# First attention with its first 128 tokens ahead, and the router's scores in two parts

## The chip, the cores and the metric

One core of a Trainium2 chip runs the kernel. The metric is device time in microseconds, the median over executions. The profile is of one further execution, and its times are counted from the start of its span. PE is TensorE, DVE is VectorE, ACT is ScalarE, POOL is GpSimd, SP is SyncE.

## What is computed

The reference takes x of 2 x 1024 x 128 through two blocks, each a mixer and a feed-forward part, with a modulated layer norm ahead of each part. All is float32.

```
h = layernorm(x)*(1+ca)+sa;  x = x + ga*spikes(h)        # RWKV-like scan, then a membrane with threshold
h = layernorm(x)*(1+cb)+sb;  x = x + gb*transformer(h)   # 2 layers: shifted tokens, 8 heads of 64, window 64, GLU
h = layernorm(x)*(1+ca)+sa;  x = x + ga*lru(h)           # second block: linear recurrence
h = layernorm(x)*(1+cb)+sb;  x = x + gb*moe(h)           # shared expert + 8 experts, top 2 by sigmoid score
q = l2norm(q)*q_scale; k = l2norm(k)*k_scale             # inside attention, then rotary with scaling
shift_token(t): features 64..127 come from the token before
```

## The kernel before

The 2,048 tokens are held feature-major (features in partitions) in four groups of 512, and token-major in 16 tiles of 128. Every engine runs one program in the order in which it is written, and semaphores tie them together. Nothing is planned at run time: an instruction that waits holds up all behind it on its engine.

The change touches two places.

**The ramp into the first attention.** VectorE has run the membrane passes and turns the membrane states into spikes with `threshold(g)` (compare, then multiply by the gate, 512 columns), groups 0 to 2 ahead of a branch on a fallback, group 3 later. `add_spikes(g)` adds them to x: groups 0 and 1 on VectorE, 2 and 3 on GpSimd. TensorE turns each group token-major (`stack_t1`). For the layer norm VectorE takes statistics (`ln_stats`: four BATCH_NORM rows, then the negated mean at L1012 and the variance plus epsilon at L1013), GpSimd computes the power -0.5 (`ln_rstd`, L715) and the negated mean times it (L716), ScalarE normalises four tiles (`ln_norm`, L412), TensorE turns them back (`ln_t2`), and ScalarE writes z with the modulation (`stack_out`, L418). For group 0 VectorE copies z into hsA, lower half straight and upper half shifted by one token (`shifted`, L1193 and L1195); DMAs do that for groups 1 to 3. From hsA, TensorE makes k and q of a tile (`proj_part`, L1596) and v (`proj_v`, L1651). VectorE makes the rotary products (L1211, L1214), ScalarE squares, VectorE sums and clamps them (L1225, L1232), and GpSimd computes the power -0.5 of the 16 sums (`norms`, L909) and scales k (`k_normed`, L917), while VectorE scales q (L1240). TensorE then turns q and k (`turn_qk`, L1507), and scores, exponentials and the product with v follow. `keep_clock(n)` is n products of constants that nothing reads.

```
proj_v(0, 0); proj_part(0, 2, 1); keep_clock(3, psT1[:, :]); turn_qk(0, 0); proj_part(0, 2, 0)
# proj_v, first tile:
pe.wait_ge(s["ln_norm"], TPG * (ln_no(1, NG - 1) + 1))
```

`norms(0)` belongs to tile 0 of the first attention. Its later tiles overlap three deep: while tile i is weighed, i+1 is scored, i+2 turned, and i+3 projected.

**The router.** After its scores are through the sigmoid, `compare_scores` compares the eight scores of each token pairwise on VectorE (is_equal and is_gt, 1,024 columns each, L1451), GpSimd combines the two results, and `weigh_experts` (L1457 to L1470, twelve VectorE steps) makes the gates. Between them VectorE makes the products of the shared expert (`shared_hidden(k)`, L1423, eight in all) for which TensorE waits, group by group, and copies each group's result (L1481). TensorE opens each group's result by turning x into it (L1971), and then adds the shared expert (L1976).

## Time and profile before

| what | us |
|---|---|
| median of 3 runs | 549.89 |
| lowest and highest | 549.76, 549.9 |
| the profiled execution | 550.24 |
| its span | 548.4 |
| PE busy, DVE busy in the span | 491.0, 424.6 |
| ACT busy, POOL busy in the span | 348.8, 339.6 |

A busy PE is not PE at its peak, since matmuls are pipelined. What counts for a change is which engine's wait ends last in the stretch that it touches, so the rows below are of stretches and not of the whole.

### The profile page before, as it was taken

How to read it: one execution, taken by the hardware profiler on the slowest of the kernel's cores; microseconds unless marked ns; L12 is line 12 of the kernel's file. 1: busy time of each engine (PE TensorE's matmuls, PEld its weight loads, DVE VectorE, ACT ScalarE, POOL GpSimd, SP SyncE). 2: the span in 40 equal slices, each digit the busy share in tenths (PEclk: the TensorE clock that was granted, in tenths of full speed). 3: DMA queues.
4: the chain of work that ended last, by engine and by line, in shares of the span. 5: the costliest groups of instructions: out<-in, count | busy, mean ns of one | idle time of the engine just before them, and what ended most of it. 6: DMA issues, size and time to landing. Idle time of an engine off the chain costs nothing.

```text
span 548.4 us, 11780 instructions
## 1 busy us (share of the span) xinstructions
PE 491.0 (90%) x4047; PEld 312.7 (57%) x4047; DVE 424.6 (77%) x1172; ACT 348.8 (64%) x999; POOL 339.6 (62%) x271
## 2 busy tenths in 40 slices
PE   5753078999999999999899999999999999999996
PEld 5333033567777776443367777777544445667775
DVE  6899999898899875566889988995545687466665
ACT  5762007689999987433689999998565536433332
POOL 5990018999999997667999999993101277410000
PEclk9875579999999999999999999999999999999999
DMA  9600003311111112000221111111000000000000
GB/s 306 232 2 1 0 2 96 68 31 41 41 40 39 39 35 78 0 1 1 70 57 39 33 40 39 41 41 31 0 2 0 1 0 1 1 1 19 22 19 20
DMA packets 15024, 20.98 MB, mean 38 GB/s; under 512 B 2378, under 2 KB 9012, under 8 KB 14708
## 3 DMA queue, kind: packets, MB, share of 16 engines
q1 hardware_dynamic: 14676, 20.13, 13.3%
q8 instruction: 33, 0.54, 0.4%
q14 instruction: 27, 0.22, 0.1%
q10 hardware_dynamic: 288, 0.08, 0.1%
HBM read 9.99 MB, written 1.05 MB: 20 GB/s over the span
## 4 chain that ended last, share of the span: by engine, by line
PE 67%; DVE 16%; POOL 8%; issue 4%; ACT 3%; DMA 1%; DVEq 0%; SPq 0%; POOLq 0%; ACTq 0%
PE psT L1507 11%; PE psQK L1596 8%; PE psO L1719 6%; PE psO L1651 5%; PE psQK L1926 5%; PE psS L1699 4%; DVE vst L1106 3%; DVE vAB L1110 3%; PE psO L1507 3%; POOL rn L909 3%; PE psS L1998 3%; PE psQK L1733 3%; PE psS L1835 3%; PE psO L1998 2%; PE psQK L1858 2%
## 5 line engine op out<-in xcount | busy, mean ns | idle before, releaser
L575 ACT ACTIVATE prob<-psS,nmx 128x128 f32<-128x128 f32 x256 | 90.1, 377 | 18.0 <-DVE nmx L1246 18.0
L909 POOL TENSOR_TENSOR rn<-ssq,half 128x16 f32<-128x16 f32 x32 | 93.2, 2912 | 6.8 <-DVE ssq L1232 6.7
L901 POOL TENSOR_TENSOR ra<-ra,rb 128x512 f32<-128x512 f32 x64 | 80.6, 1280 | 1.0 <-DVE rb L1214 0.8
L715 POOL TENSOR_TENSOR rst<-mv,half 128x4 f32<-128x4 f32 x24 | 25.7, 1072 | 73.8 <-DVE mv L1013 64.0
L1596 PE MATMUL psQK<-wqkv,hsA 128*128 128x512 f32 x128 | 61.2, 596 | 0.9 <-DVE hsA L1195 0.6
L575 ACT ACTIVATION_READ_ACCUMULATOR prob<-psS,nmx 128x1 f32 x256 | 55.1, 215 | 0.0
L917 POOL TENSOR_TENSOR qkn<-ra,rn 128x512 f32<-128x512 f32 x32 | 49.6, 1549 | 2.5
L1211 DVE TENSOR_TENSOR ra<-psQK,rope 128x512 f32<-128x512 f32 x64 | 43.9, 685 | 9.4 <-PE psQK L1596 8.9
L1214 DVE TENSOR_TENSOR rb<-psQK,rope 128x512 f32<-128x512 f32 x64 | 43.5, 679 | 0.0
L696 ACT ACTIVATE gel<-psQK 128x512 f32<-128x512 f32 x32 | 19.1, 597 | 37.5 <-PE psQK L1926 37.5
L1225 DVE TENSOR_REDUCE ssq<-sq 128x8 f32<-128x512 f32 x64 | 41.0, 676 | 1.6 <-ACT sq L515 1.3
L1246 DVE TENSOR_REDUCE nmx<-psS 128x4 f32<-128x512 f32 x64 | 41.0, 682 | 0.7 <-PE psS L1699 0.7
L1507 PEld LDWEIGHTS psT<-ident,qkn 128*128 128x128 f32 x256 | 29.6, 141 | 20.5 <-issue 14.5
L1507 PEld LDWEIGHTS psT<-ident,prob 128*128 128x128 f32 x256 | 29.9, 140 | 15.9 <-issue 15.4
L1719 PE MATMUL psO<-vAB,pT 128*64 128x64 f32 x1024 | 36.9, 225 | 0.0
L549 ACT ACTIVATE pT<-psT 128x512 f32<-128x512 f32 x64 | 36.3, 648 | 0.7 <-PE psT L1507 0.7
L1507 PE MATMUL psT<-ident,qkn 128*128 128x128 f32 x256 | 34.0, 274 | 2.6 <-DVE qkn L1240 2.0
L1719 PEld LDWEIGHTS psO<-vAB,pT 128*64 128x64 f32 x1024 | 32.4, 138 | 6.8 <-issue 4.6
L1651 PE MATMUL psO<-wqkv,hsA 128*128 128x512 f32 x64 | 35.7, 640 | 0.0
L412 ACT ACTIVATE lnx<-psS,nmr,rst 128x128 f32<-128x128 f32 x20 | 7.5, 457 | 43.6 <-POOL nmr L716 43.6
L1699 PE MATMUL psS<-kT,qT 64*64 64x128 f32 x1024 | 33.4, 269 | 0.0
L1351 DVE SCALAR_TENSOR_TENSOR hg<-psO,vec,gel 128x512 f32<-128x512 f32 (+1 forms) x24 | 17.2, 745 | 20.9 <-ACT gel L628 20.9
(262 smaller groups left out, 1183.8 us busy)
## 6 DMA issues: line engine op xcount, KB each, us to landing
vAB<-vAB SPq DMA_DIRECT2D x62, 128.0 KB, 2.2
wqkv<-in_wqkv SPq DMA_DIRECT2D x2, 768.0 KB, 8.4
big<-in_x SPq DMA_DIRECT2D x4, 256.0 KB, 4.8
ra<-in_rope_t SPq DMA_DIRECT2D x1, 1024.0 KB, 7.3
ropeb<-in_rope SPq DMA_DIRECT2D x1, 1024.0 KB, 8.6
big<-in_ew SPq DMA_DIRECT2D x2, 512.0 KB, 4.1
wmod<-in_wmod SPq DMA_DIRECT2D x2, 384.0 KB, 6.9
out<-big SPq DMA_DIRECT2D x3, 256.0 KB, 2.3
```

The costliest lines, as they stand in the source:

```text
L575: act.activation(prob[:, k, :], psS[:, hb, c * P:(c + 1) * P], ACT.Exp, bias=nmx[:, k:k + 1], accum_out=sums[:, n % 2, k:k + 1]).then_inc( ...
L901: pool.tensor_tensor(o, o, rb[:, r], ALU.add).then_inc(s["sum_" + name], 1)
L909: pool.tensor_tensor(rn[:, :], ssq[:, :], half[:, :], ALU.pow).then_inc(s["rn_ready"], 1)
L917: pool.tensor_tensor(heads(qkn[:, INNER:]), heads(ra_k[n % 2]), rn[:, 8:16].unsqueeze(2).to_broadcast([P, H, DH]), ALU.mult).then_inc(s["k ...
L1211: dve.tensor_tensor(heads(o), heads(psQK[:, part, :]), rope[:, at8, 2 * part, :].unsqueeze(1).to_broadcast([P, H, DH]), ALU.mult).then_inc ...
L1214: dve.tensor_tensor(rb[:, r].rearrange("p (h a d) -> p h a d", h=H, a=2), psQK[:, part, :].rearrange("p (h a d) -> p h a d", h=H, a=2)[:, ...
L1225: dve.tensor_reduce(ssq[:, 8 * part:8 * part + 8], heads(sq[:, part * INNER:(part + 1) * INNER]), AX.X, ALU.add).then_inc(s["ssq_" + name], 1)
L1507: i = pe.transpose(dst[:, k * P:(k + 1) * P], src(k), ident[:, :])
L1596: mm(psQK[:, part, :], hsA[:, tile(i)], wqkv[:, part * INNER:(part + 1) * INNER], start=True, stop=True).then_inc(s[name + "_mm"], 1)
L1651: mm(psO[:, 1, :], hsA[:, tile(i)], wqkv[:, 2 * INNER:3 * INNER], start=True, stop=True).then_inc(s["v_fill"], 1)
L1699: j = mm(psS[64 * w:64 * w + 64, e, c * P:(c + 1) * P], qT[r, c, 64 * w:64 * w + 64], keys, start=False, stop=True, skip_group_check=True)
L1719: j = mm(psO[64 * w:64 * w + 64, 0, h * DH:(h + 1) * DH], pT[:, slot(h), 64 * w:64 * w + 64], (vA, vB)[w][:, u, h * DH:(h + 1) * DH], star ...
```

## The change

Group 0 of the first layer norm is taken in two steps. ScalarE computes its power as exp(-0.5 ln v), normalises two tiles, and as soon as TensorE has turned the first tile (into psQK) it writes z for tokens 0 to 127; VectorE copies these into hsA, and the first k product starts from them. The other three tiles are turned behind that product, and z and hsA for tokens 128 to 511 follow. The power of tile 0's sums (`norms(0)`) moves from GpSimd to ScalarE in the same way, ahead of the normalisation of group 3; the table set with ln and exp is loaded beforehand. Thresholds 2 and 3 move from VectorE to GpSimd, each ahead of its add. Several steps of all four engines change places: ScalarE's first squares of k come ahead of group 2's normalisation, VectorE's statistics of groups 2 and 3 come later, GpSimd's rstd of group 3 comes between the two rotary sums of tile 0, and TensorE's turn of group 3 comes behind the q product. Of the ten and four clock-keeping products there, four, two and four remain.

In the router, is_gt moves behind the fourth product of the shared expert, GpSimd's multiply waits for is_equal alone, and `weigh_experts` is cut in two: seven steps (`choose_experts`) after the sixth product, five ahead of the eighth. The copy of group 2's result moves behind the eighth.

```
@@ -498,6 +498,7 @@
     act.wait_ge(s["table"], 1)
+    act.preload_act_table_set("natural_log_exp_and_others")
     load_table(ACT.Exp)
...
@@ -519,13 +520,45 @@
         ln_out(ln_no(1, g), z[:, gsl(g)], mod[:, 0, CB, b:b + 1], mod[:, 0, SB, b:b + 1])
-    ln_norm(ln_no(1, 0))
-    stack_out(0)
+    def power(dst, src):
+        own.one(act.activation(dst, src, ACT.Ln, bias=0.0, scale=1.0))
+        return act.activation(dst, dst, ACT.Exp, bias=0.0, scale=-0.5)
+    def first_norm():
+        n = ln_no(1, 0)
+        act.wait_ge(s["ln_var"], n + 1)
+        power(rst[:, n % 4, :], mv[:, n % 4, :, 1]).then_inc(s["rst_act"], 1)
+        act.wait_ge(s["rst_act"], 1)
+        act.wait_ge(s["ln_rstd"], n + 1)
+        act.wait_ge(s["ln_t2"], n - 1)
+        for k in range(TPG):
+            act.activation(lnx[:, n % 2, k, :], stat_bank(n)[:, k, :], ACT.Identity, bias=nmr[:, n % 4, k:k + 1],
+                           scale=rst[:, n % 4, k:k + 1]).then_inc(s["ln_norm"], 1)
+            if k == 1:
+                act.wait_ge(s["first_t2"], 1)
+                act.activation(z[:, 0:P], psQK[:, 0, 0:P], ACT.Identity, bias=mod[:, 0, SB, 0:1],
+                               scale=mod[:, 0, CB, 0:1]).then_inc(s["first_out"], 1)
+        act.wait_ge(s["ln_t2"], n + 1)
+        act.activation(z[:, P:GW], out_bank(n)[:, P:GW], ACT.Identity, bias=mod[:, 0, SB, 0:1],
+                       scale=mod[:, 0, CB, 0:1]).then_inc(s["ln_out"], 1)
+    def norms(n):
+        act.wait_ge(s["ssq_max"], n + 1)
+        if n:
+            act.wait_ge(s["k_ready"], n)
+            act.wait_ge(s["q_ready"], n)
+        power(rn[:, :], ssq[:, :]).then_inc(s["rn_ready"], 1)
+    first_norm()
     ln_norm(ln_no(1, 1))
+    squares_k(0)
     ln_norm(ln_no(1, 2))
     stack_out(1)
-    squares_k(0)
     squares_q(0)
+    norms(0)
     ln_norm(ln_no(1, 3))
@@ -878,16 +911,19 @@
     def add_spikes(g):
+        own.one(pool.tensor_scalar(by_chunk(ekv, g), of_group(ph, g, 1), -1.0, mod[:, 0, GA, bof(g):bof(g) + 1],
+                                   ALU.is_lt, ALU.mult))
         pool.wait_ge(s["x_mixed"], g)
-        if g == 3:
-            pool.wait_ge(s["spk"], 1)
         pool.tensor_tensor(x_cm[:, gsl(g)], x_cm[:, gsl(g)], ekv[:, gsl(g)], ALU.add).then_inc(s["x_mixed"], 1)
+    pool.wait_ge(s["x_mixed"], 1)
     add_spikes(2)
-    ln_rstd(ln_no(1, 0))
+    n = ln_no(1, 0)
+    pool.wait_ge(s["rst_act"], 1)
+    pool.tensor_tensor(nmr[:, n % 4, :], nmean[:, n % 4, :], rst[:, n % 4, :], ALU.mult).then_inc(s["ln_rstd"], 1)
     add_spikes(3)
-    for g in range(1, NG):
-        ln_rstd(ln_no(1, g))
+    ln_rstd(ln_no(1, 1))
+    ln_rstd(ln_no(1, 2))
     def heads(x):
...
@@ -921,10 +957,13 @@
         if has(i + 2):
-            norms(n + 2)
+            if n + 2:
+                norms(n + 2)
             k_normed(n + 2)
...
             rope_sum(n + 3, 1)
+            if n + 3 == 0:
+                ln_rstd(ln_no(1, 3))
             rope_sum(n + 3, 0)
...
@@ -990,8 +1029,9 @@
     pool.tensor_tensor(ew2g[0], ew2, gate(0, NE), ALU.mult).then_inc(s["wg_ready"], 1)
+    pool.wait_ge(s["pairs_ready"], 1)
+    own.one(pool.tensor_tensor(big4, big4, before[:, :, :].unsqueeze(1).to_broadcast(sh4), ALU.mult))
     pool.wait_ge(s["pairs_ready"], 2)
-    own.one(pool.tensor_tensor(big4, big4, before[:, :, :].unsqueeze(1).to_broadcast(sh4), ALU.mult))
     pool.tensor_tensor(big4, big4, big5, ALU.add).then_inc(s["better_ready"], 1)
...
@@ -1151,7 +1191,6 @@
     threshold(own, 1)
-    threshold(own, 2)
     changed = dve.value_load(cnti[0:1, 0:1], min_val=0, max_val=P * B * NCH)
...
@@ -1170,7 +1209,7 @@
         renewed = Steps(dve, s["renewed"])
-        for g in range(NG - 1):
+        for g in range(2):
             threshold(renewed, g)
...
@@ -1183,9 +1222,7 @@
     ln(ln_no(1, 0))
-    threshold(Steps(dve, s["spk"]), 3)
     ln(ln_no(1, 1))
-    ln(ln_no(1, 2))
     def shifted(dst, src, g, name):
@@ -1265,14 +1302,23 @@
         clamped(n)
+    dve.wait_ge(s["first_out"], 1)
+    dve.tensor_copy(hsA[0:64, 0:P], z[0:64, 0:P]).then_inc(s["hsA_first"], 1)
+    dve.tensor_copy(hsA[64:128, 1:P + 1], z[64:128, 0:P]).then_inc(s["hsA_first"], 1)
+    ln(ln_no(1, 2))
     dve.wait_ge(s["ln_out"], ln_no(1, 0) + 1)
-    shifted(hsA, z, 0, "hsA_ready")
+    dve.tensor_copy(hsA[0:64, P:GW], z[0:64, P:GW]).then_inc(s["hsA_ready"], 1)
+    dve.tensor_copy(hsA[64:128, P + 1:GW + 1], z[64:128, P:GW]).then_inc(s["hsA_ready"], 1)
+    dve.wait_ge(s["rope_ready"], 4)
+    rope_products(0, 1)
     ln(ln_no(1, 3))
-    dve.wait_ge(s["rope_ready"], 4)
-    qk_first(0)
+    rope_products(0, 0)
+    sum_squares(0, 1)
+    sum_squares(0, 0)
+    clamped(0)
     rope_products(1, 1)
+    q_normed(0)
     rope_products(1, 0)
-    q_normed(0)
     def mid(l, g):
@@ -1447,22 +1493,30 @@
         own.one(dve.tensor_tensor(sel, sg, rbias[:, :].unsqueeze(1).to_broadcast([P, NT, NE]), ALU.add))
-        for pairs, op in ((big4, ALU.is_equal), (big5, ALU.is_gt)):
-            dve.tensor_tensor(pairs, sel.unsqueeze(2).to_broadcast(sh4), sel.unsqueeze(3).to_broadcast(sh4),
-                              op).then_inc(s["pairs_ready"], 1)
-    def weigh_experts():
+        dve.tensor_tensor(big4, sel.unsqueeze(2).to_broadcast(sh4), sel.unsqueeze(3).to_broadcast(sh4),
+                          ALU.is_equal).then_inc(s["pairs_ready"], 1)
+    def compare_greater():
+        dve.tensor_tensor(big5, sel.unsqueeze(2).to_broadcast(sh4), sel.unsqueeze(3).to_broadcast(sh4),
+                          ALU.is_gt).then_inc(s["pairs_ready"], 1)
+    dn2 = sq[:, 3 * P + NT:3 * P + 2 * NT]
+    dn3 = sq[:, 3 * P + 2 * NT:3 * P + 3 * NT]
+    def choose_experts():
         dve.wait_ge(s["better_ready"], 1)
...
         own.one(dve.tensor_reduce(den, comb, AX.X, ALU.add))
-        dn2 = sq[:, 3 * P + NT:3 * P + 2 * NT]
-        dn3 = sq[:, 3 * P + 2 * NT:3 * P + 3 * NT]
         own.did(dve.tensor_scalar(dn2, den, 1e-9, None, ALU.is_gt))
...
         own.one(dve.reciprocal(den, den))
+    def weigh_experts():
         own.one(dve.tensor_tensor(den, den, dn2, ALU.mult))
...
@@ -1472,13 +1526,19 @@
         for k in range(max(2 * g, 2), 2 * g + 2):
+            if k == 2 * NG - 1:
+                weigh_experts()
             shared_hidden(k)
...
                 compare_scores()
+            elif k == 3:
+                compare_greater()
         if g == 2:
-            weigh_experts()
-        dve.wait_ge(s["ey_done"], g + 1)
-        dve.tensor_copy(big[:, 4, gsl(g)], (psT0, psT1)[g % 2][:, :]).then_inc(s["ey_used"], 1)
+            choose_experts()
+        else:
+            for m in ((g - 1, g) if g == NG - 1 else (g,)):
+                dve.wait_ge(s["ey_done"], m + 1)
+                dve.tensor_copy(big[:, 4, gsl(m)], (psT0, psT1)[m % 2][:, :]).then_inc(s["ey_used"], 1)
     dve.wait_ge(s["ey_used"], NG)
...
@@ -1589,7 +1649,10 @@
         name = "qk"[part]
-        stacked(l, i)
+        if n:
+            stacked(l, i)
+        else:
+            pe.wait_ge(s["hsA_first"], 2)
         if n:
...
@@ -1625,18 +1688,26 @@
     stack_t1(1)
+    keep_clock(4, psT1[:, :])
     stack_t1(2)
-    keep_clock(10, psT1[:, :])
-    ln_t2(ln_no(1, 0))
-    stack_t1(3)
+    keep_clock(2, psT1[:, :])
+    first = ln_no(1, 0)
+    pe.wait_ge(s["ln_norm"], TPG * first + 1)
+    pe.transpose(psQK[:, 0, 0:P], lnx[:, first % 2, 0, :], ident[:, :]).then_inc(s["first_t2"], 1)
     keep_clock(4, psT1[:, :])
...
     proj_part(0, 0, 1)
+    pe.wait_ge(s["ln_norm"], TPG * (first + 1))
+    for k in range(1, TPG):
+        i = pe.transpose(out_bank(first)[:, k * P:(k + 1) * P], lnx[:, first % 2, k, :], ident[:, :])
+    i.then_inc(s["ln_t2"], 1)
+    proj_part(0, 0, 0)
+    stack_t1(3)
     ln_t2(ln_no(1, 1))
-    proj_part(0, 0, 0)
+    proj_part(0, 1, 1)
     ln_t2(ln_no(1, 2))
-    proj_qk(0, 1)
+    proj_part(0, 1, 0)
     keep_clock(4, psT1[:, :])
```

## Rows read from the trace of the kernel before

**Rows 1.** The page: the chain that ended last, shares of the span by engine.
```profile
PE 67%; DVE 16%; POOL 8%; issue 4%; ACT 3%; DMA 1%; DVEq 0%; SPq 0%; POOLq 0%; ACTq 0%
```

**Rows 2.** Timeline of VectorE from 77.8 us: start, length, engine, line, operation, tiles, count, idle.
```profile
77.92 1.29 DVE L1180 TENSOR_TENSOR x_cm<-x_cm,big 128x512 f32<-128x512 f32 x2 [0.27 <-DVE big L1147]
...
80.84 0.16 DVE L1013 TENSOR_SCALAR mv<-mv 128x4 f32<-128x4 f32 x1
...
82.85 1.17 DVE L1012 TENSOR_SCALAR nmean<-mv 128x4 f32<-128x4 f32 x1
```

**Rows 3.** Timeline of GpSimd, 77.8 to 83 us.
```profile
79.36 1.26 POOL L884 TENSOR_TENSOR x_cm<-x_cm,big 128x512 f32<-128x512 f32 x1 [36.85 <-DVE x_cm L1180]
...
82.58 0.20 POOL L716 TENSOR_TENSOR nmr<-nmean,rst 128x4 f32<-128x4 f32 x1
82.73 1.26 POOL L884 TENSOR_TENSOR x_cm<-x_cm,big 128x512 f32<-128x512 f32 x1
```

**Rows 4.** The chain that ended last, 76.2 to 78.7 us: start, length, what.
```profile
77.32 0.53 issue
```

**Rows 5.** Timeline of GpSimd, 209 to 220.5 us.
```profile
209.78 3.87 POOL L826 TENSOR_SCALAR tsin<-big 128x1024 f32<-128x1024 f32 x1
...
218.96 1.16 POOL L826 TENSOR_SCALAR tsin<-big,fr 128x1024 f32<-128x1024 f32 x1
```

**Rows 6.** Timeline of VectorE in the same stretch.
```profile
209.72 0.42 DVE L1193 COPY big<-z 64x512 f32<-64x512 f32 x1
210.17 1.15 DVE L1195 COPY big<-z 64x512 f32<-64x512 f32 x1
```

**Rows 7.** Timelines of ScalarE, 5 to 22 us and 82.5 to 98 us.
```profile
12.92 0.19 ACT L474 ACTIVATE sc<-fr 128x3 f32<-128x3 f32 x1
...
82.81 1.50 ACT L412 ACTIVATE lnx<-psS,nmr,rst 128x128 f32<-128x128 f32 x4 [35.41 <-POOL nmr L716]
85.06 0.78 ACT L418 ACTIVATE z<-psO,mod 128x512 f32<-128x512 f32 x1 [0.75 <-PE psO L1507]
...
91.27 1.50 ACT L412 ACTIVATE lnx<-psO,nmr,rst 128x128 f32<-128x128 f32 x4
```

**Rows 8.** Timeline of VectorE, 104 to 113.5 us.
```profile
105.78 0.67 DVE L1232 TENSOR_SCALAR ssq<-ssq 128x16 f32<-128x16 f32 x1
```

**Rows 9.** Timeline of GpSimd, 88 to 114 us.
```profile
92.46 2.91 POOL L909 TENSOR_TENSOR rn<-ssq,half 128x16 f32<-128x16 f32 x1 [0.28 <-DVE ssq L1232]
...
106.53 2.91 POOL L909 TENSOR_TENSOR rn<-ssq,half 128x16 f32<-128x16 f32 x1
```

**Rows 10.** Timeline of TensorE, 84 to 98.5 us.
```profile
86.90 1.10 PE L1596 MATMUL psQK<-wqkv,hsA 128*128 128x512 f32 x2 [0.57 <-DVE hsA L1195]
...
93.32 1.02 PE L1651 MATMUL psO<-wqkv,hsA 128*128 128x512 f32 x2
...
97.05 0.65 PE L1507 MATMUL psT<-ident,qkn 128*128 128x128 f32 x4 [0.24 <-POOL qkn L917]
```

**Rows 11.** Timeline of VectorE, 470 to 487.5 us.
```profile
473.47 1.22 DVE L1451 TENSOR_TENSOR rb<-sq 128x1024 f32<-128x1024 f32 x1
...
483.20 0.17 DVE L1466 TENSOR_TENSOR sq<-sq 128x16 f32<-128x16 f32 x1
...
484.14 0.29 DVE L1470 TENSOR_TENSOR sq<-sq 128x128 f32<-128x128 f32 x1
...
485.08 1.28 DVE L1423 TENSOR_TENSOR hg<-psO,gel 128x512 f32<-128x512 f32 x2
```

**Rows 12.** Timeline of TensorE, 470 to 489 us.
```profile
474.07 1.02 PE L1920 MATMUL psO<-hsA,wsh 128*128 128x512 f32 x2
475.34 0.66 PE L1971 MATMUL psT<-ident,x_cm 128*128 128x128 f32 x4 [0.24 <-DVE hg L1423]
...
486.41 0.66 PE L1971 MATMUL psT<-ident,x_cm 128*128 128x128 f32 x4 [0.39 <-DVE hg L1423]
```

**Rows 13.** The chain that ended last, 468 to 490 us.
```profile
483.44 0.86 PE psS L1919 x2
```

More of the change, by code:

```diff
@@ L193, in program @@
             kv_mm num_ready ek_ready gek_ready ekv_ready sb_ready den_ready r_mm r_ready cur_ready x_mixed
-            rope_scaled rope_turned td_ready kbias halves scales eps_ready seed_ln seed_ready newton_ready rough_ready quot_ready
+            rst_act first_t2 first_out hsA_first rope_scaled rope_turned td_ready kbias halves scales eps_ready seed_ln seed_ready newton_ready rough_ready quot_ready
             dve dve_b act_own pool_own fallback fallback_b rope_ready tabs_phase tabs_ready z_ready hsA_ready
```

## The prediction

> **What bounds the kernel now.** I read the page first. The chain that ended last is two thirds TensorE [rows 1], so a gain counts only where TensorE waits. There are two such places under the change: the ramp into the first attention, and the router. Next I read the timelines of VectorE, GpSimd, ScalarE and TensorE from 77.8 us on, as one sequence. VectorE adds spikes to the first two groups from 77.92, the first being done at about 78.6 [rows 2]. GpSimd adds the third group from 79.36 to 80.62. The first group's variance is ready at 81.00; GpSimd raises it to the power -0.5 and multiplies, and ScalarE normalises from 82.81 [rows 2, 7]. TensorE turns all four tiles, ScalarE writes z from 85.06 to 85.84 [rows 7], VectorE copies it into hsA, and the first product starts at 86.90, 0.15 after the copies end at 86.75 [rows 10]. Tile 0's clamp is done at about 92.38, GpSimd's power follows from 92.46 to 95.37 [rows 9], TensorE turns tile 0's q and then its k, the latter at 97.05 [rows 10]. The reader should see which queue has something behind each wait.
>
> **Removing threshold 2 from VectorE: nothing.** The instruction is about 0.65 us, as an add of the same columns is (1.29 for two), but VectorE is already idle for 0.27 us before its first add [rows 2]. The chain shows 0.53 us of issue there [rows 4], just behind the branch on the fallback. The branch path sets the start, and the branch does not wait for threshold 2. Bounds: 0, and a gain of 0.65 if reading the branch's value turns out to queue behind it. I take 0.
>
> **Thresholds 2 and 3 on GpSimd: 1.9 us each.** No row shows this pair of operations there. The nearest are tensor-scalar instructions on 1,024 columns: 1.16 us for multiply and add, 3.87 us for add and add [rows 5]. Halved for 512 columns that is 0.58 and 1.94. Compare-and-multiply is not multiply-and-add, so I take 1.9. [...]
>
> **What that does to the first variance: +1.1.** Threshold 2 starts at 78.6 + 0.15 = 78.76 and ends at 80.66; the third add then runs to 82.0 instead of 80.62. VectorE's negated mean falls at 80.76, inside that add. The trace has the same meeting: a negated mean, as small as the variance of 0.16, took 1.17 from 82.85 and ended at 84.02, as GpSimd's add of 82.73 ended at 83.99 [rows 2, 3]. So the variance is ready at 82.1, not 81.00.
>
> **Ln and Exp for the first power: -1.0.** From variance to normalising takes 81.00 to 82.81 = 1.81 before. After, it is two small ScalarE instructions of 0.19 [rows 7], the multiply on GpSimd of 0.20 [rows 3] and 0.22 of handovers between them, 0.80 in all. Normalising starts at 82.1 + 0.8 = 82.9: the saving pays for the collision and no more.
>
> **The first 128 tokens: a product 0.45 to 2.35 us earlier.** One normalisation is 1.50 / 4 = 0.375 [rows 7], one turn with handovers about 0.35, one small z about 0.4: z's first 128 columns are there at 84.05. GpSimd is then in threshold 3 (82.9 to 84.8), with its fourth add behind it (84.85 to 86.1). The two copies to hsA are VectorE copies, and a copy beside GpSimd's 3.87 us instruction took 1.15 instead of 0.42 [rows 6]: held, but not to the end of it. Three outcomes: both pass during threshold 3 (copies done 84.4), both pass as it ends (85.05), or the second falls behind the fourth add (86.3). The product starts 0.15 later: 84.55, 85.2 or 86.45, against 86.90.
>
> **The rest of the group: later.** The three other turns now stand in TensorE's queue behind that product, and ScalarE waits for them with everything behind it. Product 0.86, turns 0.55, z for 384 columns 0.65: z is whole 2.07 after the product starts, at 86.6, 87.3 or 88.5, against 85.84. The two larger copies (0.72) end at 87.35, 88.0 or 89.25, against 86.75. From there to the clamp VectorE does the same instructions as before (the statistics of group 3, four rotary products, two sums): 92.38 - 86.75 = 5.63, so 93.0, 93.65 or 94.9.
>
> **Tile 0's power on ScalarE: 2.4 saved, and not reached.** Ln and Exp take about 0.45 instead of 2.91 [rows 7, 9]: done at 93.45, 94.1 or 95.35, against 95.37. But the normalisation of group 3 stands behind them on ScalarE (1.50), and ends at 95.0, 95.65 or 96.9, where it ended at 91.27 + 1.50 = 92.77 before [rows 7]. The first v product (93.32 before [rows 10]) waits for it, and in TensorE's queue that product, a k product and three clock-keeping products (0.86 + 0.86 + 0.65) stand ahead of the turn of q. So the turn of q comes at 97.4, 98.1 or 99.35, and that of k 0.44 behind it: 0.8, 1.45 or 2.75 later than 97.05. The saved 2.4 us lie under this wait.
>
> **What reaches the steady state: +0.3, +0.95 or +2.25.** Tile 2's power started at 106.53 as GpSimd came free [rows 9]. Its clamp was drawn out to 0.67 from 105.78 [rows 8], where so small an instruction takes 0.16 [rows 2]: 0.5 us of room. The rest passes on, since TensorE is then nearly full to the end of the layer. I take the middle of the first two, +0.6.
>
> **Router: -0.7.** TensorE is free at 474.93 (474.07 + 0.86, the step of such a product in the chain [rows 13]) and waits for VectorE's fourth product until 475.34, because the second comparison (1.22) stands ahead of that product [rows 11, 12]. With the comparison behind it, the product can start at 473.5 or as soon as its SiLU is there, 0.64 us: no wait is left, -0.41. GpSimd's multiply starts a comparison earlier, so its two results are not late. At the last group TensorE waits until 486.41. There VectorE first ends five weighing steps (483.20 to 484.43), a copy, then two products (485.08, 1.28) [rows 11]. After the change the first product starts when TensorE's third group ends (483.44 - 0.41 = 483.03 [rows 13]), then 0.64, five steps of 1.23 together, 0.68 and handovers: 485.65, and TensorE goes on at 485.7, -0.7 in all. Bounds: -0.41, and -0.41 - 0.39 = -0.8, the idle time before that row [rows 12].
>
> **Sum.** +0.6 - 0.7 = -0.1. The profiled execution took 550.24 us (548.4 of span and 1.84 around it), which gives 550.1; it stands 0.35 over the median of the runs, 549.89, so I forecast 549.8.
>
> **Rivals.**
> *Slower: the first copies fall behind the fourth add.* For it: the negated mean of 82.85 and the copy of 210.17 each let GpSimd's instruction go on [rows 2, 6]. Against it: both may slip through at 84.8. It decides if the second copy asks for its data after threshold 3 ends and the add has begun. Attention +2.25, router -0.7: +1.55, a median of 551.4, and up to 551.9 if the threshold is longer than its nearest row.
> *Faster: cheap thresholds and no held copies.* At 0.58 per threshold the third add keeps its time and the variance is ready at 81.0. Normalising starts at 81.85, z's first columns are there at 83.0, the product starts at 83.4, z is whole at 85.45, and k turns about 0.4 earlier than before. With GpSimd's 2.91 gone from the ramp, part of the 0.5 of room is gained too: about -0.6, and -1.3 with the router, 548.6. If threshold 2 did hold up the branch, another 0.65: 547.9. Cheap thresholds with the copies held behind the fourth add leave attention at 0 and the sum at -0.7, 549.2: no verdict.
> *No effect of the first 128:* that is nearly the forecast itself; the lead is lost in the rest of its group.
>
> **Chances.** Measured medians of this kernel differ by a tenth of a us, but 0.2% (1.1 us) is about what tells a change from none. Forecast, within 0.2%: 0.43 (its own range 549.2 to 550.4). Slower rival: 0.28. Faster rival: 0.29, kept high because it needs only one price to be at its lower end. The range takes in both: 547.9 to 551.9.
>
> **What would show each step.** Right: two GpSimd tensor-scalar rows of about 1.9 us at 78.8 and 82.9; a negated mean of about 1.2 us near 80.8; normalising from 82.9; a product before 86.5 but whole z after 86.5; the v product after 95; TensorE's turn for the last group some 0.7 earlier, counted from the router's start. Wrong: thresholds under 1 us; copies unharmed beside them; group 3's normalisation ending before 94.

## The result, and the profile after

The changed kernel takes 551.64 us (median of 20 runs, 550.47 to 555.0) against 549.88 for the kernel before, timed beside it (20 runs, 549.76 to 551.45). The ratio is 1.0031 with a 95% interval of 1.0023 to 1.004: slower by 0.3%, where no change was forecast.

Two things are in these numbers. The profiled execution is longer by only 0.64 us (550.88 against 550.24), and the quickest run by 0.71 (550.47 against 549.76). The median is longer by 1.76, because the times of the changed kernel spread. The clock that the chip grants to TensorE, averaged over a run as a share of full speed, is 0.961 to 0.963 in the quickest seven runs and 0.954 to 0.958 in the four longest of the 20.

First the profiled execution. The timeline of GpSimd after, from 77.5 us:

```profile
78.70 2.84 POOL L914 TENSOR_SCALAR big<-vAB,mod 128x512 f32<-128x512 f32 x1 [36.27 <-DVE x_cm L1219]
81.62 1.26 POOL L917 TENSOR_TENSOR x_cm<-x_cm,big 128x512 f32<-128x512 f32 x1
82.84 0.20 POOL L923 TENSOR_TENSOR nmr<-nmean,rst 128x4 f32<-128x4 f32 x1
83.02 2.59 POOL L914 TENSOR_SCALAR big<-vAB,mod 128x512 f32<-128x512 f32 x1
85.69 1.27 POOL L917 TENSOR_TENSOR x_cm<-x_cm,big 128x512 f32<-128x512 f32 x1
86.91 1.04 POOL L748 TENSOR_TENSOR rst<-mv,half 128x4 f32<-128x4 f32 x1
...
107.72 2.91 POOL L945 TENSOR_TENSOR rn<-ssq,half 128x16 f32<-128x16 f32 x1 [1.86 <-DVE ssq L1269]
```

The two thresholds take 2.84 and 2.59. No idle time is noted between the first six rows: for 8.2 us GpSimd only works off its queue. The third add starts 2.26 later than before [rows 3], and everything small behind a long row is late by that row. Group 0's product with its power (L923) and group 1's power (L748) are the two that others wait for. VectorE and ScalarE show who:

```profile
77.82 1.29 DVE L1219 TENSOR_TENSOR x_cm<-x_cm,big 128x512 f32<-128x512 f32 x2 [0.87 <-DVE big L1187]
...
80.67 0.17 DVE L1052 TENSOR_SCALAR nmean<-mv 128x4 f32<-128x4 f32 x1
80.74 0.16 DVE L1053 TENSOR_SCALAR mv<-mv 128x4 f32<-128x4 f32 x1
...
82.15 0.76 DVE L1052 TENSOR_SCALAR nmean<-mv 128x4 f32<-128x4 f32 x1
...
84.66 0.22 DVE L1306 COPY hsA<-z 64x128 f32<-64x128 f32 x1 [1.68 <-ACT z L541]
84.91 0.23 DVE L1307 COPY hsA<-z 64x128 f32<-64x128 f32 x1
...
87.83 0.36 DVE L1311 COPY hsA<-z 64x384 f32<-64x384 f32 x1
...
93.66 0.18 DVE L1269 TENSOR_SCALAR ssq<-ssq 128x16 f32<-128x16 f32 x1
```

```profile
81.18 0.20 ACT L526 ACTIVATE rst<-rst 128x4 f32<-128x4 f32 x1
83.12 0.81 ACT L537 ACTIVATE lnx<-psS,nmr,rst 128x128 f32<-128x128 f32 x2 [1.74 <-POOL nmr L923]
...
88.28 1.50 ACT L412 ACTIVATE lnx<-psS,nmr,rst 128x128 f32<-128x128 f32 x4 [0.87 <-POOL nmr L749]
...
94.12 0.22 ACT L526 ACTIVATE rn<-rn 128x16 f32<-128x16 f32 x1
94.24 1.49 ACT L412 ACTIVATE lnx<-psO,nmr,rst 128x128 f32<-128x128 f32 x4
```

The first power is there at 81.38 and lies idle until 83.12. Group 1 is normalised at 88.28, where before it was at 85.74:

```profile
85.74 1.50 ACT L412 ACTIVATE lnx<-psS,nmr,rst 128x128 f32<-128x128 f32 x4
```

Tile 0's power on ScalarE takes 0.47 and is done at 94.34, but group 3's normalisation behind it ends at 95.73. TensorE after, in the same stretch:

```profile
82.93 0.66 PE L1567 MATMUL psT<-ident,x_cm 128*128 128x128 f32 x4 [2.24 <-POOL x_cm L917]
...
85.28 1.10 PE L1659 MATMUL psQK<-wqkv,hsA 128*128 128x512 f32 x2 [0.29 <-DVE hsA L1307]
...
89.84 0.66 PE L1567 MATMUL psO<-ident,lnx 128*128 128x128 f32 x4 [1.84 <-ACT lnx L412]
...
95.87 1.10 PE L1722 MATMUL psO<-wqkv,hsA 128*128 128x512 f32 x2 [0.94 <-ACT lnx L412]
...
98.31 1.04 PE L1567 MATMUL psT<-ident,qkn 128*128 128x128 f32 x8
```

The wait in the first of these rows, 2.24 us for the third group's spikes, was 0.75 before:

```profile
80.67 0.66 PE L1507 MATMUL psT<-ident,x_cm 128*128 128x128 f32 x4 [0.75 <-POOL x_cm L884]
```

The first product comes 1.62 earlier than before [rows 10], the first v product 2.55 later. The turn of k (the second half of the last row, at 98.75) is 1.7 later, and tile 2's power 1.19 (107.72 against 106.53 [rows 9]).

The end of the router, first TensorE, then GpSimd, then VectorE:

```profile
487.05 0.66 PE L2042 MATMUL psT<-ident,x_cm 128*128 128x128 f32 x4 [0.28 <-DVE hg L1469]
```

```profile
474.84 2.36 POOL L1033 TENSOR_TENSOR ra<-ra,before 128x1024 f32<-128x1024 f32 x1 [5.88 <-DVE ra L1496]
...
480.74 2.35 POOL L1036 TENSOR_TENSOR big<-big,osb 128x1024 f32<-128x1024 f32 x1
```

```profile
475.63 2.65 DVE L1501 TENSOR_TENSOR rb<-sq 128x1024 f32<-128x1024 f32 x1
...
482.19 0.99 DVE L1511 TENSOR_SCALAR sq<-sq 128x128 f32<-128x128 f32 x1
...
484.43 0.69 DVE L1469 TENSOR_TENSOR hg<-psO,gel 128x512 f32<-128x512 f32 x1
...
486.30 0.69 DVE L1469 TENSOR_TENSOR hg<-psO,gel 128x512 f32<-128x512 f32 x1
```

TensorE's last turns start 0.64 after those of before (486.41 [rows 12]), while the first attention had passed 1.20 on: the router gives back 0.56.

A ruler for all that follows: the stage from VectorE's first add of spikes (L1180 before) to tile 0's scaled output (`osb`). It is 33.59 before (77.92 to 111.50) and 34.87 after (77.82 to 112.69): +1.28. The two outputs, before and after:

```profile
111.50 0.69 DVE L1255 TENSOR_TENSOR osb<-psO,orc 128x512 f32<-128x512 f32 x1
```

```profile
112.69 0.69 DVE L1292 TENSOR_TENSOR osb<-psO,orc 128x512 f32<-128x512 f32 x1
```

From the last such output to the end of the span it is 158.69 and 158.12: -0.57. These two make the 0.7 of the quickest runs. In every kernel of this study without the router's edit the second number is 158.7, and in every one with it 158.1.

### The profile page after: what moved, and what is told of

Its sections match the earlier page's. It is cut to its first block, busy times and chain, and to the rows that moved or that the text cites. A ratio compares the mean times of both kernels' runs of the same rounds, so it can differ in the third digit from the quotient of the medians.

```text
span 549.1 us, 11778 instructions
## 1 busy us (share of the span) xinstructions
PE 488.3 (89%) x4043; PEld 312.6 (57%) x4043; DVE 425.2 (77%) x1172; ACT 349.5 (64%) x1004; POOL 340.4 (62%) x271
## 3 DMA queue, kind: packets, MB, share of 16 engines
HBM read 9.99 MB, written 1.05 MB: 20 GB/s over the span
## 4 chain that ended last, share of the span: by engine, by line
PE 65%; DVE 17%; POOL 8%; issue 4%; ACT 4%; DMA 1%; DVEq 0%; SPq 0%; POOLq 0%; ACTq 0%
PE psT L1567 10%; PE psQK L1659 8%; PE psO L1790 6%; PE psO L1722 5%; PE psQK L1997 5%; PE psS L1770 4%; DVE vst L1146 3%; DVE vAB L1150 3%; PE psO L1567 3%; PE psS L2069 3%; PE psQK L1804 3%; PE psO L2069 2%; PE psQK L1929 2%; PE psS L1906 2%; POOL rn L945 2%
## 5 line engine op out<-in xcount | busy, mean ns | idle before, releaser
L945 POOL TENSOR_TENSOR rn<-ssq,half 128x16 f32<-128x16 f32 x31 | 90.3, 2913 | 8.6 <-DVE ssq L1269 8.6
L748 POOL TENSOR_TENSOR rst<-mv,half 128x4 f32<-128x4 f32 x23 | 24.2, 1053 | 72.2 <-DVE mv L1053 62.4
L953 POOL TENSOR_TENSOR qkn<-ra,rn 128x512 f32<-128x512 f32 x32 | 48.5, 1516 | 3.2 <-ACT rn L526 0.8
L1567 PE MATMUL psT<-ident,prob 128*128 128x128 f32 x256 | 33.2, 273 | 0.0
```

The source lines that it names most:

```text
L945: pool.tensor_tensor(rn[:, :], ssq[:, :], half[:, :], ALU.pow).then_inc(s["rn_ready"], 1)
L953: pool.tensor_tensor(heads(qkn[:, INNER:]), heads(ra_k[n % 2]), rn[:, 8:16].unsqueeze(2).to_broadcast([P, H, DH]), ALU.mult).then_inc(s["k ...
L1567: i = pe.transpose(dst[:, k * P:(k + 1) * P], src(k), ident[:, :])
```

## The experiments

The expectations count groups from one: their second group is group 1 of the kernel, their fourth is group 3. The changed kernel's first 20 runs are in the section above. Stages are of the profiled execution. Kernels under one heading ran on one chip with runs of the kernel before beside them, unless said.

| kernel | runs | median | quickest | stage |
|---|---|---|---|---|
| before | 135 | 549.8 to 549.9 | 549.55 | 33.59 |
| router alone | 12 | 549.39 | 549.11 | 33.59 |
| change without router | 9 | 552.6 | 551.15 | 34.88 |
| change, later waits filled | 12 | 551.23 | 550.51 | 34.85 |
| before, 8 clock products fewer | 12 | 550.45 | 549.85 | 33.58 |
| change, all waits filled | 12 | 551.2 | 550.39 | 34.88 |
| change, no clock products | 10 | 552.19 | 551.51 | 36.60 |
| thresholds on VectorE | 12 | 549.12 | 548.88 | 33.36 |
| group 3's normalisation first | 12 | 551.44 | 549.78 | 35.52 |
| both of these | 11 | 549.47 | 548.38 | 32.85 |
| powers and router alone | 5 | 547.39 | 547.33 | 31.86 |
| threshold 3 alone on GpSimd | 11 | 549.19 | 549.0 | 33.56 |
| change, long wait filled | 11 + 11 | 550.49, 550.64 | 550.4 | 34.84, 34.86 |
| change again | 5 | 551.71 | 550.65 | 34.84 |
| both, waits filled | 12 | 549.16 | 548.44 | 32.87 |

### Which half costs, and do clock-keeping products matter?

*Router alone:* the router's part of the change put into the kernel before.

> The kernel before with the router's edit alone. Theory: the router gives back 0.56 us (its last turns start 0.64 after the kernel before's, while the attention passed 1.20 on), and the spread of the changed kernel's times (550.5 to 555.0 at mean granted clocks of 0.963 down to 0.954) comes from the ramp into the first attention. Then this kernel takes 549.3, as tight as the kernel before (within about 0.3 us). Rival: the spread comes from the router's new order; then these runs spread over several us as well, and the mean granted clock moves with them.

549.39, ratio 0.999 [0.9981, 0.9998]; ten of 12 runs between 549.11 and 549.53. The gain of about 0.5 is the router's, and the spread is not.

*Change without router:* the same part taken out of the changed kernel.

> The changed kernel without the router's edit. Theory: the attention's part costs 1.2 us in executions whose granted clock is the best one, so the quickest runs are at 551.0 to 551.2 (0.56 above the changed kernel's quickest), and the runs spread upwards by up to 4 us, the mean granted clock going down with them; median about 552.2. Rival (spread from the router): all runs within 0.4 us of 551.1.

The runs fall into three clusters: 551.15 to 551.19 (clock 0.962, 0.963), 552.5 to 552.8 (0.960), 554.1 to 554.3 (0.952 to 0.957). As the theory has it, the ramp carries both the loss and the spread.

*Later waits filled:*

```diff
             stack_t1(3)
+            keep_clock(8, psT1[:, :])
             ln_t2(ln_no(1, 1))
             proj_part(0, 1, 1)
+            keep_clock(4, psT1[:, :])
             ln_t2(ln_no(1, 2))
             proj_part(0, 1, 0)
-            keep_clock(4, psT1[:, :])
+            keep_clock(8, psT1[:, :])
```

> The changed kernel with 16 more clock-keeping products in three waits of TensorE in the ramp: 8 before the turns of the second group, 4 before those of the third, 4 more before the first v product. Each takes 0.21 us, and the three waits are 1.84, 0.97 and 0.94 us long, so nothing waits for them. Theory (TensorE stands idle in these waits, and in some executions its clock is then granted at 1.2 GHz for a stretch): the spread is gone, all runs at 550.5 to 550.9, mean clock 0.961 to 0.963 in each. Rival (the spread has another cause, such as the order of VectorE and GpSimd, which changes from run to run): runs still spread to 553 and above, with the clock.

In the profile of this run a clock product follows the last by 0.216 us: eight take 1.89 (from 87.51) and four 1.03 (from 91.03), each record being 0.38 long itself. They delay nothing: from the first product to the turns of group 1 it is 4.56 (84.95 to 89.51), as in the changed kernel (85.28 to 89.84), to the v product 10.58 against 10.59, and the stage is 34.85 against 34.87. What the expectations call 1.2 GHz is a granted clock of 0.50 of full speed in the profiles, which give the clock as that share alone.

The theory missed: six of 12 runs are at 550.51 to 550.75, four at 551.7 to 551.8, two at 553.6 with a clock of 0.952 and 0.956. The spread is there, as the rival said, though the rival's own cause is not shown by it. Filling these three waits is not enough.

*Before, 8 clock products fewer:* the two `keep_clock(4)` ahead of the first k and the first v product removed.

> The kernel before without 8 clock-keeping products: the 4 ahead of the first product of the attention and the 4 ahead of the first v product. Work that the result needs is unchanged. Theory (the clock falls where TensorE stands idle in the ramp): the shortest run stays at about 549.8, others are 1 to 4 us longer, with lower mean clocks, as in the changed kernel. Rival: the 8 products do nothing there, all runs at 549.7 to 550.2.

Neither outcome: the runs go from 549.85 to 551.5, but the longer ones have clocks of 0.960 to 0.966, like the shorter. In the profile (550.92) the stage is 33.58, as before, and the first add comes at 78.47 instead of 77.92, so in this execution the missing products cost the stage nothing. Yet 7 of 12 runs are over 550.4, against 5 of 32 of the kernel before beside it; whether the products matter in the long runs stays open. The profile shows another source of spread: among all the profiles, whose code up to the adds differs by threshold 2 at most, the first add stands at 77.35 to 78.47.

### The long wait, the thresholds, the order on ScalarE

*All waits filled:* the edit of the run with the later waits filled, and `keep_clock(12)` instead of `keep_clock(4)` behind `stack_t1(1)`.

> The changed kernel with the 16 added clock-keeping products of the run before this one, and 8 more in the longest of TensorE's waits in its ramp: the 2.24 us from 80.69 to 82.93 in which it waits for the third group's spikes (0.75 us in the kernel before). 8 products take 1.72 us. Theory (the idle time in the ramp lowers the clock in some executions): the quickest runs stay at 550.5, and no more runs lie over 551.0 than of the kernel before (about 1 in 8). Rival (the spread has a cause other than TensorE's idle time): half of the runs over 551.5 still.

Inconclusive. The long end is gone (552.26 at most), and only one run is over 551.5, where the rival wanted half. But seven of 12 runs are over 551.0, where the theory allowed one in eight; they lie 0.8 to 1.9 over the quickest at clocks of 0.961 to 0.965. Ten of 33 runs of the kernel before beside it were over 550.4 too.

*No clock products:* the four calls (4, 2, 4, 4) removed.

> The changed kernel without the 14 clock-keeping products between the first turns of the ramp and the first v product (4, 2, 4 and 4). Work that the result needs is unchanged. Theory (idle time in the ramp lowers the clock): most runs are 1.4 to 6 us over 550.5, with a mean granted clock of 0.960 or less, and a profile of it would show a stretch at 1.2 GHz somewhere behind 77 us. Rival (another cause): the same spread as the changed kernel, with a third of the runs still at 550.5 to 550.9.

No run under 551.5; clocks 0.949 to 0.958. The trace has TensorE's clock at 0.50 of full speed from 81.9 to 88.7 (0.99 from 79.5 to 81.9), beginning within a wait of 3.1 us (79.54 to 82.64), and the stage is 1.73 longer than that of the changed kernel.

*Thresholds on VectorE:*

```diff
             def add_spikes(g):
-                own.one(pool.tensor_scalar(by_chunk(ekv, g), of_group(ph, g, 1), ...
                 pool.wait_ge(s["x_mixed"], g)
+                if g == 3:
+                    pool.wait_ge(s["spk"], 1)
...
             threshold(own, 1)
+            threshold(own, 2)
...
             ln(ln_no(1, 0))
+            threshold(Steps(dve, s["spk"]), 3)
             ln(ln_no(1, 1))
```

> The changed kernel with both thresholds back on VectorE, at the places they have in the kernel before; the rest of the change stays. Theory (the 2.85 and 2.59 us that they take on GpSimd delay the third and the fourth add and the second group's power, and that is what the attention lost): the first product starts at about 83.6 instead of 85.28, the second group's normalisation at about 86 instead of 88.28, the turn of tile 0's q about 1.7 earlier than 98.31, and the quickest runs take 548.9. Rival (what was lost lies in the queue of ScalarE: the fourth group's normalisation behind tile 0's power): the turn of q moves by less than 0.5, and the quickest runs take 550.1 to 550.5.

As the theory has it: 549.12, ratio 0.9984 [0.9973, 0.9994], quickest 548.88, 11 of 12 runs within a microsecond. GpSimd and ScalarE in this kernel:

```profile
78.98 1.26 POOL L917 TENSOR_TENSOR x_cm<-x_cm,big 128x512 f32<-128x512 f32 x1 [36.84 <-DVE x_cm L1219]
81.18 0.20 POOL L922 TENSOR_TENSOR nmr<-nmean,rst 128x4 f32<-128x4 f32 x1 [0.94 <-ACT rst L526]
81.38 1.26 POOL L917 TENSOR_TENSOR x_cm<-x_cm,big 128x512 f32<-128x512 f32 x1
```

```profile
81.47 0.81 ACT L537 ACTIVATE lnx<-psS,nmr,rst 128x128 f32<-128x128 f32 x2 [0.36 <-POOL nmr L922]
...
85.53 1.50 ACT L412 ACTIVATE lnx<-psS,nmr,rst 128x128 f32<-128x128 f32 x4
```

GpSimd now waits for ScalarE and not the other way round, and group 1 is normalised 2.75 earlier, of which 0.28 is an earlier first add (77.54). The wait of 2.24 us is gone as well, and most of the spread with it.

*Group 3's normalisation first:* `norms(0)` and `ln_norm(ln_no(1, 3))` change places on ScalarE.

> The changed kernel with the fourth group's normalisation ahead of tile 0's power on ScalarE, as it stood in the kernel before; the thresholds stay on GpSimd. Theory (the first v product waits for that normalisation, and the turns of tile 0 stand behind that product): the normalisation starts as the square of q ends, 92.85 instead of 94.24, the v product at 94.4 instead of 95.87, the turn of q at about 97.0 instead of 98.31, and the quickest runs take 549.3 (1.2 under the changed kernel's 550.5). Rival (the delay made on GpSimd ahead of it sets the turns by another road, so that nothing is won by this order): the quickest runs stay at 550.3 to 550.6.

The quickest run is 549.78: 0.7 won, not 1.2. In its profile the rotary products of tile 1 and the copies of v, q and k behind them follow on the chain. Half of the runs are over 551.7, at clocks down to 0.953, and this time the profiled execution (551.09) was a longer one. Two stretches of it, by span, busy times and then the granted clock (third from the end):

```profile
80.00:83.60 3.60, 1.36 (x10) 0.85 (x9) 2.48 (x16) 1.22 (x4) 3.52 (x4) 1.00 0.01 2
83.60:87.05 3.45, 3.45 (x9) 1.37 (x7) 2.25 (x12) 1.15 (x3) 3.37 (x3) 0.51 0.00 0
```

The second in the changed kernel:

```profile
83.60:87.05 3.45, 3.16 (x14) 1.54 (x13) 2.26 (x12) 1.79 (x5) 3.37 (x3) 1.00 0.00 0
```

And its TensorE there:

```profile
82.54 0.65 PE L1567 MATMUL psT<-ident,x_cm 128*128 128x128 f32 x4 [2.23 <-POOL x_cm L917]
...
83.57 1.84 PE L1670 MATMUL psT<-masks,identb 128*128 128x512 bf16 x4
85.20 1.92 PE L1659 MATMUL psQK<-wqkv,hsA 128*128 128x512 f32 x2
```

From 83.64 to 87.05 the granted clock is 0.50, behind the wait of 2.23 us. Four clock products take 1.84 (1.03 at 79.28, where the clock is 1.00), the first product 1.92 (1.10 [rows 10]). It falls on the chain, and the run is 1.31 over the quickest.

### What each part is worth

*Both of these:* the two edits above together.

> The changed kernel with both thresholds back on VectorE and with the fourth group's normalisation ahead of tile 0's power. Theory (two delays in two queues that add up: GpSimd's thresholds, 1.6 us in the quickest runs, and ScalarE's order, 0.7): 548.2 in the quickest runs, and no spread, since the wait of 2.24 us of TensorE is gone. Rival (with the thresholds gone the clamp of tile 0 sets the turns alone, and the order on ScalarE no longer matters): 548.8 to 549.0, as with the thresholds moved back alone.

Quickest 548.38, near the theory's 548.2: the delays add up. The other half of the theory missed: the long wait is gone, but seven of 11 runs lie 1.0 to 1.7 over the quickest, up to 550.1. So ending that wait does not by itself end the spread.

*Powers and router alone:* the kernel before with the router's part, Ln and Exp on ScalarE for the first power and for tile 0, and `q_normed(0)` ahead of tile 1's q. Group 0 goes whole.

```diff
+            act.wait_ge(s["ln_var"], ln_no(1, 0) + 1)
+            power(rst[:, ln_no(1, 0) % 4, :], mv[:, ln_no(1, 0) % 4, :, 1]).then_inc(s["rst_act"], 1)
+            act.wait_ge(s["rst_act"], 1)
             ln_norm(ln_no(1, 0))
...
             ln_norm(ln_no(1, 3))
+            norms(0)
```

> The kernel before with the router's edit and the two powers on ScalarE alone: the first group goes whole, as before, the thresholds are on VectorE, the fourth group's normalisation stands ahead of tile 0's power. It differs from the run before this one only by the first 128 tokens, and by the order on VectorE and TensorE that goes with them. Theory (a lead of the first product is worth nothing, since tile 0's rotary products wait for VectorE, which first has the rest of the group): within 0.3 us of that run, 548.0 to 548.5. Rival (the first 128 tokens win their lead): 0.8 to 1.5 us slower than that run.

Both missed, on the other side: 547.39, ratio 0.9949 [0.9936, 0.9963], five runs within 0.2 us. It is 1.05 quicker than the run with the first 128 tokens ahead. It beats both kernels. VectorE here, the second copy to hsA and the clamp:

```profile
84.90 0.43 DVE L1217 COPY hsA<-z 64x512 f32<-64x512 f32 x1
...
90.78 0.18 DVE L1254 TENSOR_SCALAR ssq<-ssq 128x16 f32<-128x16 f32 x1
```

The same in the run with both edits:

```profile
85.90 0.36 DVE L1312 COPY hsA<-z 64x384 f32<-64x384 f32 x1
...
91.71 0.18 DVE L1270 TENSOR_SCALAR ssq<-ssq 128x16 f32<-128x16 f32 x1
```

From the end of the copies to the clamp both take 5.45. VectorE has no idle time in between in either. So the rest of the group sets the clamp, and the 128 tokens ahead make it 0.93 later: two more copies, one more z, and three turns that stand behind the first product. The order of steps on the four engines that goes with the 128 tokens was not tried apart from them.

*Threshold 3 alone on GpSimd:* the fourth group's stays there, the third group's goes back.

> The changed kernel with only the fourth group's threshold on GpSimd; the third group's is back on VectorE. Theory: the fourth threshold alone (2.6 us) holds up the second group's power, so that its normalisation starts at about 86.7 (85.53 with both on VectorE, 88.28 with both on GpSimd): 549.6 to 550.0 in the quickest runs, and no spread over a us, since the long wait of TensorE came from the third group's threshold. Rival (it lies beside other work): 548.9, as with both on VectorE.

549.19, quickest 549.0, spread of 1.1: 0.1 to 0.2 over both on VectorE, which ran on another chip. The theory had 549.6 to 550.0, so the rival is nearer. Group 1 is normalised at 86.55, as forecast and 1.02 later than with both on VectorE (85.53), yet the stage is only 0.20 longer. So the delay of group 1 is nearly covered, and what threshold 2 costs comes by group 0's product. One pair of rows is of use below, a small step of VectorE within the threshold:

```profile
81.19 2.54 POOL L915 TENSOR_SCALAR big<-vAB,mod 128x512 f32<-128x512 f32 x1
```

```profile
81.70 0.71 DVE L1052 TENSOR_SCALAR nmean<-mv 128x4 f32<-128x4 f32 x1
```

*Long wait filled:* `keep_clock(12)` instead of 4 behind `stack_t1(1)`, nothing else.

> The changed kernel with 8 more clock-keeping products in one place, TensorE's wait of 2.24 us for the third group's spikes; the other waits stay empty. Theory (the stretch at 1.2 GHz from 83.64 to 87.05 in the profile of the run with the fourth group's normalisation first comes from that wait alone): the quickest runs at 550.5, hardly any over 552.0, median about 550.8. Rival (the later waits of 1.84, 0.97 and 0.94 us lower the clock too): a third of the runs at 552 to 555, as in the changed kernel.

As the theory has it: ten of 11 runs at 550.40 to 550.63. Its profile too has a stretch at half the clock (0.50), but a later one, behind the wait of 1.84:

```profile
90.20:93.60 3.40, 3.23 (x7) 1.44 (x8) 3.18 (x11) 2.37 (x7) 2.74 (x4) 0.50 0.22 66
```

This cost nothing: the stage is 34.84 and the run 550.40. TensorE's waits for ScalarE there shrank instead (0.97 to 0.17, 0.94 to 0.29).

### Side by side

*Change again and long wait filled again*, on one chip:

> The changed kernel once more, on the same chip as the two runs after it, so that the filled wait is compared with the empty one side by side. Theory (granted clock in the ramp, from the wait of 2.24 us): quickest run at 550.4 to 550.5, half of the runs over 551.5, the mean granted clock of these lower. Rival (the spread belongs to the chip or the hour, not to the kernel): as tight as the kernel with the filled wait.

> The kernel with 8 more clock-keeping products in the wait of 2.24 us, on the same chip as the changed kernel. Theory: 550.4 to 550.7 in nearly all runs, median about 1.1 us under that of the changed kernel beside it. Rival: the same distribution as beside it.

Median 551.71 against 550.64, the difference that the theory had. Two of its signs missed: the clocks of the changed kernel's longer runs (0.960, 0.961) are not lower than that of its quickest (0.958), and only six of 11 filled runs are at 550.4 to 550.7. Of all runs of the changed kernel 16 of 25 are over 551.0, of this filled one 6 of 22. Counting the runs with the later waits filled too, it is 22 of 37 with the long wait empty and 13 of 34 with it filled. What is left need not come from the ramp: of the kernel before 28 of 135 runs are over 550.4.

*Both, waits filled:* `keep_clock` of 4, 3 and 4 in the three waits left.

> The kernel with the thresholds on VectorE and the fourth group's normalisation first (548.4 at its quickest, but 7 of 11 runs 0.9 to 1.7 us over that), with 4, 3 and 4 clock-keeping products in the three waits of 0.86, 0.76 and 0.97 us that TensorE still has in the ramp. Theory (these waits lower the clock in some executions as the longer one did): quickest runs at 548.4, most within 0.4 of it. Rival (that spread comes from ahead of the adds, where the profiles of kernels with the same code differ by up to 1.1 us): as without the products.

Neither, quite: six runs at 548.44 to 549.02, five at 549.3 to 549.7, one at 550.63. The profiled execution was one of the second kind, and its stage is 32.87, as short as without the products. What it lost lies between the two layers:

```profile
273.30:276.75 3.45, 3.45 (x10) 2.11 (x9) 2.65 (x6) 2.51 (x8) 2.95 (x3) 0.51 0.37 96
```

There TensorE had waited 1.88 us (271.07 to 272.95), and the time between the first and the last output of the layers is 279.40 instead of 278.2 to 278.4. That code is the same in all the kernels, and the run without these products had the same wait of 1.88 there and a clock of 1.00 behind it, where this one has 0.51.

## Why the prediction was wrong

Two steps failed. The thresholds on GpSimd were priced too low and without the small instructions behind them in that queue, so the attention lost 1.2 us where +0.6 was forecast. And the longer wait that they make for TensorE was put at nothing; the other 1.1 us of the median are spread, which went where this wait alone was filled. The router's term was off by 0.13. Step by step:

**Removing threshold 2 from VectorE: nothing.** Right. The adds start 0.10 earlier, which is within the scatter of that start between profiles (77.35 to 78.47, the earliest with threshold 2 on VectorE).

**Thresholds at 1.9 us each.** Mis-sized: 2.84 and 2.59. The row nearest to it for the price (3.87 for 1,024 columns [rows 5]) was the right one of the two and still too low. The other row, halved to 0.58, is off by a factor of more than four for a compare and multiply.

**The first variance: +1.1.** The step that failed first, in its mechanism. The longer threshold moved the add behind VectorE's negated mean (0.17 at 80.67), and the variance came at 80.90, not 82.1. The loss came by a road that the working did not follow: GpSimd's own queue. The product of mean and power stands behind threshold 2 and the third add, so ScalarE's quick power (right: 0.44 from 80.94 to 81.38) waited 1.74 us. Normalising started at 83.12; forecast 82.9.

**The first 128 tokens.** 85.28 lies in the range of 84.55 to 86.45. The copies passed beside threshold 3 at 0.22 and 0.23, not held, as in the first outcome, but late, so in the second outcome's time (85.14; it had 85.05). That the middle one fits is luck: z's first columns came at 84.63 instead of 84.05, and the copies were not held. Two sizes in that working were estimates with no row beside them: the small z, put at about 0.4, took 0.46 (from 84.17), and the turn, put at 0.35 with its handovers, 0.27 without them (from 83.86).

**The rest of the group.** z whole 87.41, larger copies until 88.19, clamp done at 93.84 (forecast for the middle outcome: 87.3, 88.0, 93.65). What it missed is group 1: its power stood behind threshold 3 and the fourth add and its normalisation came 2.54 later than before. That the sizes agree is partly luck, but that the rest of the group pays is shown: without the 128 tokens, and the order that goes with them, the stage is 0.99 shorter.

**Tile 0's power: saved and not reached.** Right in mechanism and size: group 3's normalisation ends at 95.73 (95.65), and putting it first won 0.5 (thresholds on VectorE) to 0.7.

**What reaches the steady state: +0.6.** Mis-sized: +1.28 by the stage, +1.2 on the clock of the run. The times of the middle outcome came, and it had 0.95; the mean of it and a better one was taken without a row that spoke for the better. The room of 0.5 was right (1.7 at the turn, 1.19 at tile 2's power).

**Router: -0.7.** Mis-sized by 0.13: -0.57. TensorE goes on behind its third group at 484.02, 0.74 later than before (483.28), where the attention had passed 1.20 on: 0.46 won, with 0.41 forecast. The last wait gave only 0.10 more, with 0.29 forecast. A SiLU, put at 0.64, takes 0.60 on ScalarE (before, 473.19 and 474.27). The second comparison, now beside GpSimd's multiply (474.84 to 477.20), took 2.65 instead of 1.22 [rows 11], and still came in time. But among the seven steps that choose the experts one took 0.99 from 482.19, until GpSimd's next multiply ended at 483.09 (0.51 before, at the end of the same multiply), so the next product starts at 484.43, 0.4 behind the end of TensorE's third group, and the last at 486.30.

**What was not in the working at all.** The change leaves TensorE idle for 2.24 us where it was idle for 0.75. The working counted idle time of TensorE only where it lies on the chain, and put this wait at nothing. Of the 1.76, 0.7 is the work's order, shown part by part; the other 1.1 or so is the spread of the times. Filling this wait alone takes 1.07 off the median side by side, and 1.15 against the first 20 runs, and leaves the stage as it was (34.84, 34.86). With the later waits filled as well it takes off the longest runs (553.59 to 552.26 at most) but nothing off the median (551.23 to 551.2). So the runs tie the spread to this wait in part, and not beyond doubt.

That the clock is how the wait costs is argued, not shown. For it: the profile of the run with group 3's normalisation first has a stretch at a clock of 0.50 behind this wait, and that run is 1.31 over the quickest; the kernel without clock products has one twice as long that begins in it. Against it: the two kept profiles of the changed kernel (550.88 and 550.65) are of quick runs and have a clock of 1.00 there (83.6 to 87.05), and no long run of it was profiled. The mean clocks do not settle it either. TensorE's clock on the pages of the kernel before and of the changed kernel, in tenths over 40 equal slices, and on that of the run with group 3's normalisation first:

```profile
PEclk9875579999999999999999999999999999999999
```

```profile
PEclk9975579999999999999999999999999999999999
```

```profile
PEclk9966588999999999999999999999999999999999
```

The means of these three executions are 0.958, 0.963 and 0.961. The lowest belongs to the kernel before, by a stretch at 0.50 between 17 and 22 us (18.2 to 21.1), long before the ramp, and every profile has a mean clock of only 0.50 to 0.58 over 34 to 76 us. So the mean of a run does not tell where its clock was low.

**The slower rival.** The median of 551.64 lies where this rival put it (551.4 to 551.9), and that is luck: its reason, copies that fall behind the fourth add, did not occur.

The five parts, by the stage: the two powers -1.73, the first 128 tokens +0.99, tile 0's power ahead of group 3's normalisation +0.51, threshold 3 on GpSimd +0.20, threshold 2 on GpSimd +1.31. The sum is +1.28. Each is the difference of two profiles, taken in the order of the list, and the second holds the order of steps that goes with the 128 tokens. The large gain was there, and the other parts of the change spent it.

Open: what the clock was in the changed kernel's long runs, why the runs with all waits filled and those with both edits spread as they do, and how much of each kernel's spread is the stretch between the layers and how much the start.

## What to carry to other kernels

Price a moved operation at the queue that it moves into: list every small instruction behind it there, and who waits for each. Sending part of a group ahead pays only if what waits next needs just that part; here the rest of the group came later by what the lead cost. When a change lengthens a wait of TensorE, compare the times of many runs, with the wait empty and filled, and profile a long one: one profile can miss what most runs lose, and a run's mean clock does not say where the clock was low.

## What the runs showed of the hardware

- TensorE's granted clock fell to 0.50 of full speed within a wait of 3.1 us (no clock products), and to 0.50 or 0.51 behind waits of 1.84 (long wait filled), 1.88 (both, waits filled) and 2.23 us (group 3's normalisation first); behind waits of the same lengths it stayed at 1.00 in other profiles (1.84 in the second profile of the long wait filled, 1.88 in that of both edits, 2.24 in the changed kernel's). So the place of a fall varied from one profile to the next. The run was 1.31 us over the quickest of its kernel where TensorE set the pace (83.64 to 87.05), the time between the layers' outputs was 1.0 to 1.2 longer with the stretch between the layers (273.3 to 276.75), and the stage was no longer where TensorE waited for ScalarE anyway (90.2 to 93.6; 34.84).
- Clock products, whose records are 0.38 us long, came 0.216 us apart at a clock of 1.00: 4 took 1.03, 8 took 1.89 (later waits filled) and 12 took 2.75 (long wait filled).
- Beside GpSimd's thresholds the changed kernel's VectorE copies and first negated mean were not held (0.22, 0.23, 0.17), but elsewhere small steps were: a negated mean took 0.71 with threshold 3 alone on GpSimd, a copy beside threshold 3 took 0.57 in the kernel without clock products. Beside adds of two tensors the negated mean was held (0.76 at 82.15, until the add ended), and beside a multiply of two tensors the second comparison in the router was (2.65 for 1.22).
- Compare and multiply on 512 columns took 2.52 to 2.84 us on GpSimd, and 0.68 to 0.72 on VectorE.
